# Graph kernel on one core: the node stage's attention product computed by GpSimd instead of VectorE

## What is computed

```python
x3 = _layernorm(x2 + _leaky(neigh + self_msg))        # third layer, 128 columns
z2 = jnp.concatenate([h[src], h[dst], ex], axis=1)    # h is x3
a  = leaky_relu(z2 @ w_attn.T, negative_slope=0.01)   # fourth layer, a softmax over a follows
```

## Time and profile before

| | us |
|---|---|
| median of 3 runs | 3603.18 (3602.86 to 3603.41) |
| profiled execution, own time | 3606.04 |
| its span, first to last instruction | 3604.0 |
| DVE busy over the span | 2602.9 (72%) |
| dense node stage, edge groups (1190 to 1545) | 355 |
| dense node stage, plain nodes (1545 to 1700) | 155 |

### The profile page before, as it was taken

One profiled execution on the slowest core, in us unless ns is written; L12 is line 12 of the kernel. 1 busy time (PEld: TensorE's weight loads), 2 busy tenths in 40 slices (PEclk: granted clock), 3 DMA queues, 4 the chain that ended last, 5 costly groups with the idle time before them and its releaser, 6 DMA issues. The chain is left out here.

```text
span 3604.0 us, 57246 instructions
## 1 busy us (share of the span) xinstructions
PE 2523.9 (70%) x14627; PEld 1907.0 (53%) x14627; DVE 2602.9 (72%) x7782; ACT 2013.2 (56%) x5963; POOL 2052.6 (57%) x1978
## 2 busy tenths in 40 slices
PE   5377744999476777697687787777767757877430
PEld 2133322666355565575466666555557757776430
DVE  8689963444597899998366677798868759878542
ACT  0034322777222888798466677688867748865110
POOL 7767774774000433342777577577467767710776
PEclk9799986999799988999899899888889979987555
DMA  3455557776299444432566677677589879933221
GB/s 94 106 147 153 154 151 165 248 243 205 86 328 273 141 147 147 135 92 77 174 212 199 190 244 247 217 239 240 181 252 269 241 237 290 284 121 112 86 89 42
DMA packets 521868, 653.93 MB, mean 181 GB/s; under 512 B 99208, under 2 KB 292294, under 8 KB 521544
## 3 DMA queue, kind: packets, MB, share of 16 engines
q1 hardware_dynamic: 455242, 548.98, 48.8%
q0 software_dynamic: 65856, 100.90, 10.3%
q10 hardware_dynamic: 446, 0.40, 0.0%
HBM read 436.87 MB, written 241.92 MB: 188 GB/s over the span
## 5 line engine op out<-in xcount | busy, mean ns | idle before, releaser
L1620 POOL DMA_INDIRECT look<-table_d,ids x196 | 196.1, 1000 | 603.8 <-DVEq L1596 559.7
L1945 POOL DMA_INDIRECT xg_c<-r_d,src_row x392 | 410.9, 1048 | 167.9 <-issue 117.1
L2703 POOL DMA_INDIRECT out<-x_f,out_row x196 | 202.9, 1035 | 177.3 <-DVE x_f L2769 118.5
L1945 POOL DMA_INDIRECT xg_c<-x1d_d,src_row x196 | 216.8, 1106 | 104.8 <-issue 59.5
L1945 POOL DMA_INDIRECT xg_c<-x2d_d,src_row x196 | 203.5, 1038 | 113.0 <-issue 59.2
L925 POOL DMA_INDIRECT xd<-in_x,ids x196 | 217.6, 1110 | 71.0 <-issue 51.7
L1945 POOL DMA_INDIRECT xg_c<-g1d_d,src_row x196 | 204.7, 1044 | 79.6 <-issue 59.5
L554 POOL DMA_INDIRECT rows_d<-row,slot_i x196 | 194.1, 990 | 69.4 <-issue 55.8
L2059 ACT ACTIVATE term_c<-xg_c,scale 128x128 f32<-128x128 f32 x392 | 125.1, 391 | 181.3 <-DMA xg_c<-x1d_d,src_row 107.6
L1964 DVE TENSOR_TENSOR_SCAN agg_t_c<-flags_c,agg_t_c,term_t_c 128x512 f32<-128x512 bf16 x96 | 122.9, 1281 | 104.7 <-ACT term_t_c L2043 59.9
L1964 DVE TENSOR_TENSOR_SCAN agg_t_c<-flags_c,agg_t_c,t_ps_c 128x512 f32<-128x512 bf16 x144 | 183.2, 1273 | 1.0 <-PE t_ps_c L2366 1.0
(11 more groups left out here) (483 smaller groups left out, 8896.0 us busy)
## 6 DMA issues: line engine op xcount, KB each, us to landing
flags_c<-cont_d SPq DMA_DIRECT2D x245, 128.0 KB, 4.4
xm<-rows_d SPq DMA_DIRECT2D x49, 512.0 KB
m_d<-m_c SPq DMA_DIRECT2D x98, 256.0 KB
r_d<-r_c SPq DMA_DIRECT2D x98, 256.0 KB
m_in_c<-m_d SPq DMA_DIRECT2D x98, 256.0 KB
e_c<-rows_d SPq DMA_DIRECT2D x98, 256.0 KB
x_f<-in_x SPq DMA_DIRECT2D x67, 256.0 KB, 4.9
out<-x_f SPq DMA_DIRECT2D x67, 256.0 KB
```

The source lines that it names most:

```text
L1620: pool.indirect_dma_start(out=look[:, t, :], out_offset=None, in_=table_d[:, :], in_offset=bass.IndirectOffsetOnAxis(ap=ids[:, 0, t:t + 1] ...
L1945: pool.indirect_dma_start(out=xg[:, s, k, :], out_offset=None, in_=table, in_offset=bass.IndirectOffsetOnAxis(ap=src_row[:, t:t + 1], axis=0),
L2703: pool.indirect_dma_start(out=out[:, :], out_offset=bass.IndirectOffsetOnAxis(ap=out_row[:, t:t + 1], axis=0), in_=x4[:, n % SF, k, :], in ...
```

## The change

Product and row sums of the edge groups leave their places in `dense_dve`. The product is made by POOL in a new function, into one of two buffers of dotw (it had one, on DVE). POOL waits for u (added_u), and that the row sums of two groups before are done. The row sums stay on DVE, but stand one iteration later, for group it-8, between x1 and shift; shift waits for them. DVE also waits, ahead of u of group g, for the product of group g-3, since u has three buffers. The look-ups stay on POOL behind the product of the same iteration.

```diff
@@ dense_dve, group it - 7
+                    if g >= 3 and edge(g - 3):
+                        dve.wait_ge(attended.sem, attended.at(g - 2))
                     dve.wait_ge(halved.sem, halved.at(g + 1))
...
-                    if edge(g):
-                        dve.tensor_tensor(dotw[:, :, :], u[:, g % 3, :, :], a0[:, :, :], ALU.mult).then_inc(own.one(), 1)
                     done()
...
-                    if edge(g):
-                        dve.tensor_reduce(dotk[:, g % 2, :], dotw[:, :, :], AX.X, ALU.add).then_inc(own.one(), 1)
@@ dense_dve, group it - 8
                     if edge(g):
+                        dve.wait_ge(attended.sem, attended.at(g + 1))
+                        dve.tensor_reduce(dotk[:, g % 2, :], dotw[:, g % 2, :, :], AX.X, ALU.add).then_inc(attended_sum.sem, 1)
+                        dve.wait_ge(attended_sum.sem, attended_sum.at(g + 1))
@@ new, on POOL
+            def dense_pool(pool, it):
+                g = it - 7
+                if 0 <= g < GROUPS:
+                    pool.wait_ge(added_u.sem, added_u.at(g + 1))
+                    if g >= 2:
+                        pool.wait_ge(attended_sum.sem, attended_sum.at(g - 1))
+                    pool.tensor_tensor(dotw[:, g % 2, :, :], u[:, g % 3, :, :], a0[:, :, :], ALU.mult).then_inc(attended.sem, 1)
+                if 1 <= it < NG:
+                    pool.wait_ge(spread_ok.sem, spread_ok.at(it))
+                    for t in range(TILES * (it - 1) // (NG - 1), TILES * it // (NG - 1)):
+                        pool.indirect_dma_start(
...
```

More of the change, by code:

```diff
@@ L1317, in graph_kernel @@
             g1o = sb("g1o_n", [P, 2, K, D], F32, st)
-            dotw = sb("dotw_n", [P, K, D], F32, st)
+            dotw = sb("dotw_n", [P, 2, K, D], F32, st)
             dotk = sb("dotk_n", [P, 2, K], F32, st)
@@ L1341, in graph_kernel @@
             summed_2, added_u = signal("summed_2"), signal("added_u")
+            attended, attended_sum = signal("attended"), signal("attended_sum")
             spread_ok, rooted_n, inv_ready, normed = signal("spread_ok"), signal("rooted_n"), signal("inv_ready"), signal("normed")
@@ L1596, in dense_dve @@
                     dve.sem_inc(spread_ok.sem, 1)
+            def dense_pool(pool, it):
[9 more added lines that the diff above has]
+                        pool.indirect_dma_start(
+                            out=look[:, t, :], out_offset=None, in_=table_d[:, :],
+                            in_offset=bass.IndirectOffsetOnAxis(ap=ids[:, 0, t:t + 1], axis=0),
+                            bounds_check=TABLE - 1, oob_is_err=False).then_inc(looked.sem, 16)
             with ExitStack() as ps, nc.Block() as block:
@@ L1616, in _ @@
                 def _(pool):
[L1617 to L1623, removed]
+                    for it in range(NG + LAG):
+                        dense_pool(pool, it)
                     pool.wait_ge(looked.sem, looked.at(TILES))
@@ L1647, in graph_kernel @@
             retire([(looked, TILES), (setup, 1), (spread_ok, NG + 7), (rooted_n, NG + 7), (inv_ready, NG + 7), (normed, NN)])
-            retire([(s, GROUPS) for s in (sloped_g, x1s_ready, x2s_ready, turned_g, g1o_ready)])
+            retire([(s, GROUPS) for s in (sloped_g, x1s_ready, x2s_ready, turned_g, g1o_ready, attended, attended_sum)])
             retire([(x_in[s], len(range(s, NG, 6))) for s in range(6)] + [(x4_out[s], len(range(s, NN, 3))) for s in range(3)])
```

## The result

| | before | changed |
|---|---|---|
| median of 5 runs, us | 3603.18 (3602.86 to 3604.27) | 3583.89 (3580.43 to 3590.40) |
| profiled execution / its span | 3606.04 / 3604.0 | 3583.89 / 3582.2 |
| edge iteration 10 to 50, half_u to half_u | 7.25 | 6.90 |
| half_u of iteration 7 to half_u of iteration 57 | 360.56 | 342.87 |

The ratio of the means is 0.9949, 95% interval 0.9934 to 0.9963. By the medians the change is 19.3 us faster, where 23.5 were forecast and the range reached from 3575 to 3590. The time lies just outside the 3577 to 3583 that the prediction had worked out, in the part of its range that it had set aside for rival 1.

What follows compares the result with a forecast made beforehand. DVE was taken to bound the edge iterations; 0.59 + 0.57 - 0.69 = 0.47 us each made 24.0 us with the ends, less 0.5 charged for lateness: 23.5 us off 3603.18, so 3579.7 us. Range 3575 to 3590 us.

Steps and rivals of the forecast that it cites:

- rival 1: Edge iterations: ACT or PE partly take over as the bound; every third losing 0.4 us gives 3586 us; chance 0.11.
- DVE is the bound and stays it: Edge iterations: DVE alone sets the period, which goes from 7.25 to 6.78 us.
- The product's slot, 0.59 us: Between bn_stats and bn_aggr on DVE: removing the product shortens 1.50 us to 0.91, gain 0.59 us per iteration.
- The row sums' old place, 0.57 us: Between bn_aggr and reciprocal on DVE: without row sums 0.87 us becomes 0.30, gain 0.57 us per iteration.
- The row sums' new place, 0.69 us: Ahead of shift on DVE: row sums last 0.65 us, plus 0.04 us until waiting shift starts, cost 0.69 us.
- Both at nothing: DVE's added waits, ahead of u and ahead of the row sums: each claimed to cost nothing.
- The sum: One edge iteration: 0.59 + 0.57 - 0.69 = 0.47 us gained, period 7.25 to 6.78 us.
- POOL: Product on POOL takes 1.1 us, bounds 0.56 to 2.27; a full round with look-ups 5.5 us, so no bound.
- Who is late next: half_u waiting for lk from PE and ACT: thinnest cover 0.85 us, 0.38 us stays; 0.5 us charged in total.
- Rival 2: DVE instructions are held while POOL reads the product's two inputs; chances 0.04 for (a) and 0.05 for (b).
- (a): DVE's shift, 128x4 spread and y2, two SBUF inputs, are held at worst 0.32 us each: 3595 us; chance 0.04.
- (b): DVE's x1, one input in PSUM, is held too: 0.9 us, net loss 0.43 us per iteration, 3624 us; chance 0.05.

Runs made afterwards that it cites:

- e3: Kernel before with only the row sums moved ahead of shift, product still on DVE: period 7.38 us, whole time 3608.41 us (3596.07 before, same chip).
- e8: Changed kernel with POOL's look-ups issued only behind y2 of the same iteration: period 6.86 us, whole time 3587.25 us (3600.84 before).
- e1: Changed kernel without the added wait ahead of u: period 6.83 us, whole time 4301.33 us, ratio to before 0.9944.
- e2: Kernel before with one more long-passed wait ahead of u: period 7.32 us, whole time 3604.31 us (3596.07 before on its chip).
- e6: Kernel before with one more long-passed wait ahead of g1_t: period 7.25 to 7.26 us, whole time 4323.63 us (4311.14 before).
- e7: Changed kernel with POOL making the product twice, once into an unread spare buffer: period 6.86 us, whole time 3588.63 us.
- e5: Changed kernel with POOL's product also waiting for x1: period 7.43 us, whole time 3609.04 us (3596.07 before, same chip).
- e4: Changed kernel without the wait ahead of u, row sums back ahead of the reciprocal, one iteration later: period 6.70 us, ratios to before 0.9886, 0.9956, 0.9918.

## Why the prediction was right, and where it wasn't

- **DVE is the bound and stays it**: right. Its period is as constant as before, at a new value, 6.90 us, on chips whose whole times differ by 700 us.
- **The product's slot, 0.59 us**: right, bn_stats to bn_aggr is 0.91 us. Reading the plain nodes gave this to 0.01 us, where the product's own length would have said 0.71.
- **The row sums' old place, 0.57 us**: right, and the reciprocal's slot gave 0.02 more (0.23 for 0.25).
- **The row sums' new place, 0.69 us**: 0.71 measured, since they last 0.67 there and not 0.65. That shift itself would be longer was missed: shift to spread 0.19 against 0.13, of which 0.01 is the order on DVE (e3) and 0.05 a look-up that starts beside it (e3, e8). The prediction asked what the product would meet and put nothing down for what the look-ups, shifted by it, would meet.
- **"Both at nothing", the added waits**: the step that failed most. The wait ahead of u costs 0.07 us (e1 takes it away, e2 adds it to the kernel before). It was argued that DVE's queue reads it while half_u runs, so that it costs nothing; ahead of g1_t an added wait does cost nothing (e6), here it doesn't hold. The wait ahead of the row sums costs nothing: they start 0.61 us behind x1, as shift did before.
- **The sum**: 0.47 - 0.07 - 0.06 - 0.02 + 0.02 = 0.34, measured 7.25 - 6.90 = 0.35 us. Iterations 10 to 50 gained 14.3 us instead of 19.5, which is 5.2 of the 6.3 us between 24.0 and 17.7. Another 0.7 us are missing in iterations 51 to 53; 0.4 of them are a copy of 128x4 in iterations 51 and 52 that lasts 0.39 us instead of 0.16, until a look-up beside it is nearly over. It does so in all three profiles of the changed kernel.
- **POOL**: 1.27 us instead of 1.1, well inside the bounds (the prediction's other estimate, 1.35 us, was nearer), and the look-up behind it started after 0.15 us, not 0.84 (the earlier trace rows has a memset of 3072 columns ahead, the wrong neighbour). The start 0.1 us behind u's end came from no row; it measured 0.09. None of this mattered, as e7 shows with twice the work.
- **Who is late next**: right. No edge iteration before the 54th waited for lk, and the 0.5 us charged for it weren't needed; one iteration of 7.27 us (the 25th) has half_u 0.37 us late with nothing that the profile names. It is no scatter: the 25th is that much longer in all three profiles of the changed kernel and in e5, e7 and e8, and in e1 and e4, whose VectorE program is a wait or more shorter per iteration, it is the 21st. What happens there isn't shown.
- **Rival 2**: the mechanism of (a) exists (e5, e7) and (b), x1, doesn't (e7, and the late product of iteration 47). What kept the change clear of it is the order: the product lies beside bn_stats, bn_aggr and the reciprocal, none of which is longer than before. The list of what can be held was too short: the small tensor_scalar and copy instructions with one SBUF input can be (e8, e5, e4).
- **The whole time**: 3583.89 against 3579.7. It looks nearer than it is: the stage gave 17.7 us instead of 24, and unedited stages gave the rest of the 19.3 us, 1.6 us by the medians and 4 us in the profiled pair. That it lies in the range is in part luck: the band from 3583 up was there for rival 1, ACT or PE as the bound, and nothing of that was seen in the edge iterations.

## What to carry to other kernels

When an engine is the bound of a loop, the price of an edit is a difference of slots (start to start) between two places of the trace, not a duration; and the reader of a moved result belongs at a distance from it, with something independent between (e4, 0.13 us per iteration over e1). Before adding a wait that "has long been passed", ask whether an earlier wait covers it already; this one was covered and cost a fifth of the gain. Work given to an idle GpSimd has to be put beside VectorE instructions that a run or row has shown not to be held; here these were bn_stats, bn_aggr, the reciprocal, a tensor_reduce, and a tensor_tensor with one input in PSUM. Held were a scalar_tensor_tensor with two SBUF inputs and a small tensor_scalar with one. The same product, 2.2 us later in the iteration, turned the gain of 0.35 us into a loss of 0.18. And leave room for one that comes late: a pause of over 3 us of GpSimd, once in this stage, was harmless only by 0.39 us.

## What was not expected of the hardware

A semaphore wait that is long passed costs VectorE 0.07 us ahead of one instruction and nothing ahead of another. A look-up issued by GpSimd lengthened a 128x4 VectorE instruction with two SBUF inputs by 0.04 us, and beside one that was running 128x4 instructions with one SBUF input took 0.29 and 0.39 us instead of 0.16. A 128x4 instruction with two SBUF inputs was held 2.4 us by two products of GpSimd that it has no data in common with, and one with a single SBUF input 1.06 us by one. GpSimd paused over 3 us ahead of one and the same look-up in every kernel and on every chip, and the changed kernel's VectorE lost 0.37 us in its 25th iteration on all three chips that ran it. And the same kernel took 3584 us on one chip and 4301 us on another, while the period of a loop bound by VectorE was 6.90 us on both.
